# VectorE's order in the last two steps: the maximum of tile 31 behind the low parts of tile 29, the multiply of tile 31 behind the low parts of tile 30

## The chip, the cores and the metric

The kernel runs on one core of one Trainium2 chip. The metric is the device time in microseconds of one execution; before the change its median is 170.57 over three runs (170.32 to 170.78).

## The reference

The input x is 4 images of 128 channels by 1024 pixels, float32. Two blocks follow each other, both with a residual:

```
L0 (no softmax):  g, theta = W x + b  (64 channels)     phi = W x + b  (64 channels)
                  y = (theta^T phi / 1024) g            x1 = x + out_w y + out_b
L1 (attention):   theta, phi = W x1 + b  (128 channels)
                  attn = softmax(theta^T phi / sqrt(128))   over the 1024 pixels
                  out = x1 + conv1_w (attn x1) + conv1_b
```

## The kernel before, in words

L0 has no softmax, so the kernel folds it into one affine map per image (jobs pg, MT, R, A), and Z = x1 comes from one product (job Z). In L1 the weights of theta and phi are joined (job t makes the queries), and conv1 is multiplied into the values (job V), so that the attention yields the result but for bias and residual.

Every product that needs float32 accuracy is done in parts: a tensor is split into a high part (rounded to fp32r) and a low part (the rest), and three products high x high, high x low, low x high are added up (`three`, L220). ScalarE or GpSimd make the high parts, VectorE most of the low ones.

The attention runs in ALL = 32 tiles of 128 rows, 8 for each image, numbered 0 to 31 through the four images. For tile n these steps follow, each on its engine:

1. TensorE: scores (L223 to L225) into `ring[:, n % 2]`, two banks for each of two tiles.
2. VectorE: `row_max` (L680), the negated maximum of each row of `ring`.
3. GpSimd: `row_shift` (L821), adds a row term: the shift of the exponentials. 128x1 elements.
4. ScalarE: `exps` (L523), exponentials with their row sums, into one of 4 buffers P.
5. VectorE: `norm` (L686 and L688), reciprocal of the sums and the multiply of P, 128x1024 in place.
6. TensorE: `turn` (L318), eight transposes of 128x128 into `turned`, in two halves. It waits for `norm` of its tile and, for each half, for the low parts of the tile before (`turned` is a single buffer).
7. ScalarE: `high_turned` (L531), the high part of each half.
8. VectorE: `low_turned` (L695), the low part of each half: `turned` less the high part.
9. TensorE: `attend` (L338), for each group of four tiles, 24 products of 512 columns in four pieces, spread over the steps behind.

There is no scheduler: the order on each engine is the order in which its function issues instructions, and semaphores with constant counts join the engines. Each engine has a loop over n = 0 to 30, called steps here. A step n holds scores of tile n + 2 and transposes of tile n on TensorE; maximum of n + 2, norm of n + 1 and low parts of n on VectorE; high copies of n and then exponentials of n + 2 on ScalarE; shift of n + 2 on GpSimd. In the last image no work for a next image is left between them.

The end differs from the rest. Behind the last pieces of group 6, TensorE waits for both low parts of tile 30 and does `attend_last` for the 384 columns of tiles 28 to 30 (L345, three products for each of 8 chunks): the first two chunks, then the transposes of tile 31, then the other six. Tile 31 itself is not split into parts; it is copied once (L627 by ScalarE, L775 by VectorE) and multiplied in plain float32 (L467). `finish_last` (L703) adds bias and Z, and two DMAs store the last results. ScalarE copies the sums of group 6 (`copy_numer`, L541) behind the high copies of tile 30, and GpSimd's `finish` (L837) adds Z to that copy, 128x512, and a DMA stores it.

Of the kernel before, what the change touches and what calls it, by code (L numbers as in the profile page):

```python
# [18 lines left out]
ALL = IMAGES * TILES  # L19
# [55 lines left out]
def build(nc, x, pg_weights, pg_bias, inner, weights, out):  # L75
    with ExitStack() as ctx:
# [85 lines left out]
        def columns(half):  # L162
            return slice(half * BANK, (half + 1) * BANK)

        def half_chunks(half):
            return slice(half * CHUNKS_PER_HALF, (half + 1) * CHUNKS_PER_HALF)
# [465 lines left out]
        def _(dve):  # L632
# [21 lines left out]
            def low_t(b, half):  # L654
                dve.wait_ge(aux_high, high_after(b, f"t{half}"))
                nc.vector.scalar_tensor_tensor(out=t_lo[:, b % 2, columns(half)], in0=aux[:, :], scalar=u,
                                               in1=t_hi[:, b % 2, columns(half)].bitcast(F32), op0=ALU.add,
                                               op1=ALU.subtract).then_inc(aux_free, 1)
# [18 lines left out]
            def row_max(n):  # L677
                b, t = divmod(n, TILES)
                dve.wait_ge(scores_ready, n + 1)
                nc.vector.tensor_reduce(negmax[:, t:t + 1], ring[:, n % 2, :], AX.X, ALU.max,  # L680
                                        negate=True).then_inc(max_ready, 1)

            def norm(n):
                t = n % TILES
                dve.wait_ge(probs_ready, n + 1)
                nc.vector.reciprocal(rden[:, t:t + 1], den[:, t:t + 1]).then_inc(rden_ready, 1)  # L686
                dve.wait_ge(rden_ready, n + 1)
                nc.vector.tensor_scalar(P[:, n % P_BUFFERS, :], P[:, n % P_BUFFERS, :],  # L688
                                        rden[:, t:t + 1], None, ALU.mult).then_inc(probs_normed, 1)

            def low_turned(n, half):
                group, k = divmod(n, GT)
                rows = slice(k * TILE, (k + 1) * TILE)
                dve.wait_ge(turned_hi, n * HALVES + half + 1)
                nc.vector.tensor_tensor(PT_lo[:, group % GROUPS, half_chunks(half), rows],  # L695
                                        turned[:, columns(half)].rearrange("p (j r) -> p j r", j=CHUNKS_PER_HALF),
                                        PT_hi[:, group % GROUPS, half_chunks(half), rows].bitcast(F32),
                                        ALU.subtract).then_inc(turned_lo, 1)
# [42 lines left out]
            def early_job(b, t):  # L741
                if t == 0 and b > 1:
                    make_pg(b, 0)
                if t == 2:
                    low_A(b)
                if t == 4:
                    low_t(b, 0)
                if t == 5:
                    low_V(b, 1)
                if t == 6:  # L750
                    low_t(b, 1)

            def late_job(b, t):
                if t == 0 and b > 1:
                    make_pg(b, 1)
                if t == 4:
                    low_V(b, 0)
                if t == 5:
                    low_V(b, 2)

            for n in range(ALL - 1):
                b, t = divmod(n, TILES)
                if t and b + 1 < IMAGES:
                    late_job(b + 1, t - 1)
                if n + 2 < ALL:
                    row_max(n + 2)
                if n == 0:
                    low_t(0, 1)
                norm(n + 1)
                if n and b + 1 < IMAGES:  # L770
                    early_job(b + 1, t)
                low_turned(n, 0)
                low_turned(n, 1)
            dve.wait_ge(turned_ready, ALL * HALVES)
            nc.vector.tensor_copy(PT_last[:, half_chunks(1), :], turned[:, columns(1)].rearrange(  # L775
                "p (j r) -> p j r", j=CHUNKS_PER_HALF)).then_inc(last_turned[1], 1)
# [129 lines left out]
```

## Time and profile before

| | |
|---|---|
| median of three runs | 170.57 us |
| profiled execution, its own time | 170.84 us |
| its span | 169.0 us |
| TensorE busy (matmul) | 161.8 us, 96% |
| VectorE busy | 124.1 us, 73% |
| ScalarE busy | 95.8 us, 57% |
| GpSimd busy | 69.1 us, 41% |
| granted TensorE clock | full in all 40 slices |

The span runs from the first to the last instruction that the profiler records on the core; the execution's own time is 1.84 us longer. Busy shares are averages over the whole kernel. The ends of matmuls are modelled, so starts are the better measure on TensorE.

### The profile page before, as it was taken

What the parts mean: (1) busy time and instruction counts of PE and PEld (TensorE: products, weight loads), DVE (VectorE), ACT (ScalarE), POOL (GpSimd) and SP (SyncE); (2) the same over time, 40 slices, a digit from 0 to 9 for tenths busy, and PEclk for the clock granted to TensorE, in tenths of its full rate; (3) what the DMA queues carried; (4) which work ended last, traced back from release to release, by engine and by line L of the source; (5) the groups of instructions that cost most, each with busy time, mean ns of one, the idle gap of its engine ahead of it and who ended that gap; (6) DMA issues with size and microseconds to landing.
All of it is one profiled execution on the core that took longest, in us unless ns stands there. A gap on an engine that the chain in (4) does not pass through costs nothing.

```text
span 169.0 us, 2605 instructions
## 1 busy us (share of the span) xinstructions
PE 161.8 (96%) x967; PEld 135.2 (80%) x967; DVE 124.1 (73%) x211; ACT 95.8 (57%) x181; POOL 69.1 (41%) x79
## 2 busy tenths in 40 slices
PE   7889899799999999999999999999999999998994
PEld 7777778687888887887888888887888888886893
DVE  1316599869888876867888987667888898888412
ACT  3024558769557546567557656467566766576410
POOL 1009765277102295236415296216525253825030
PEclk9999999999999999999999999999999999999999
DMA  4603030000000010000001010000000110000111
GB/s 134 207 0 128 0 124 0 0 0 2 6 0 0 4 62 0 0 0 4 0 0 47 17 66 0 0 0 4 0 2 0 63 49 17 0 0 0 62 63 65
DMA packets 2829, 4.76 MB, mean 28 GB/s; under 512 B 448, under 2 KB 1280, under 8 KB 2816
## 3 DMA queue, kind: packets, MB, share of 16 engines
q1 hardware_dynamic: 2304, 4.39, 7.5%
q10 hardware_dynamic: 512, 0.20, 0.5%
q8 instruction: 8, 0.13, 0.3%
q14 instruction: 5, 0.04, 0.1%
HBM read 2.49 MB, written 2.10 MB: 27 GB/s over the span
## 4 chain that ended last, share of the span: by engine, by line
PE 84%; DVE 7%; DMA 3%; ACT 2%; POOL 2%; issue 1%; SPq 0%; ACTq 0%
PE numer L338 22%; PE turned L318 14%; PE ring L223 9%; PE ring L225 8%; PE ring L224 8%; PE aux L282 4%; DMA X<-x_dram 3%; DVE negmax L680 3%; PE aux L229 3%; PE aux L345 2%; PE aux L235 2%; PE aux L223 2%; DVE P L688 2%; ACT P L523 1%; PE aux L225 1%; PE aux L224 1%
## 5 line engine op out<-in xcount | busy, mean ns | idle before, releaser
L821 POOL TENSOR_SCALAR shift<-negmax,rho 128x1 f32<-128x1 f32 x32 | 27.6, 863 | 72.8 <-DVE negmax L680 69.8
L680 DVE TENSOR_REDUCE negmax<-ring 128x1 f32<-128x1024 f32 x32 | 39.1, 1223 | 19.0 <-PE ring L225 18.8
L523 ACT ACTIVATE P<-ring,shift 128x1024 f32<-128x1024 f32 x32 | 35.8, 1119 | 9.9 <-POOL shift L821 9.8
L695 DVE TENSOR_TENSOR PT_lo<-turned,PT_hi 128x512 fp32r<-128x512 f32 x62 | 39.7, 681 | 0.4 <-ACT PT_hi L531 0.4
L531 ACT ACTIVATE PT_hi<-turned 128x512 fp32r<-128x512 f32 x62 | 33.6, 595 | 9.4 <-PE turned L318 9.3
L318 PE MATMUL turned<-identity,P 128*128 128x128 f32 x256 | 33.6, 274 | 0.6 <-DVE PT_lo L695 0.6
L318 PEld LDWEIGHTS turned<-identity,P 128*128 128x128 f32 x256 | 29.5, 141 | 3.9 <-DVE P L688 1.0
L223 PE MATMUL ring<-Z_hi,t_hi 128*128 128x512 f32 x64 | 26.5, 414 | 0.9 <-DVE t_lo L725 0.7
L225 PE MATMUL ring<-Z_lo,t_hi 128*128 128x512 f32 x64 | 25.2, 394 | 0.0
L224 PE MATMUL ring<-Z_hi,t_lo 128*128 128x512 f32 x64 | 25.2, 393 | 0.0
L688 DVE TENSOR_SCALAR P<-P,rden 128x1024 f32<-128x1024 f32 x32 | 24.1, 754 | 1.1
L338 PE MATMUL numer<-PT_hi,V_hi 128*128 128x512 f32 x56 | 24.4, 436 | 0.0
L338 PE MATMUL numer<-PT_hi,V_lo 128*128 128x512 f32 x56 | 22.1, 394 | 0.0
L338 PE MATMUL numer<-PT_lo,V_hi 128*128 128x512 f32 x56 | 22.1, 394 | 0.0
L223 PEld LDWEIGHTS ring<-Z_hi,t_hi 128*128 128x128 f32 x64 | 12.0, 188 | 4.1 <-DVE t_lo L725 1.0
L225 PEld LDWEIGHTS ring<-Z_lo,t_hi 128*128 128x128 f32 x64 | 12.0, 188 | 2.7
L224 PEld LDWEIGHTS ring<-Z_hi,t_lo 128*128 128x128 f32 x64 | 12.1, 188 | 2.2
L338 PEld LDWEIGHTS numer<-PT_hi,V_lo 128*128 128x128 f32 x56 | 10.5, 188 | 2.6
L338 PEld LDWEIGHTS numer<-PT_lo,V_hi 128*128 128x128 f32 x56 | 10.6, 190 | 1.3
L338 PEld LDWEIGHTS numer<-PT_hi,V_hi 128*128 128x128 f32 x56 | 10.6, 189 | 1.3
L837 POOL TENSOR_TENSOR result<-attended,Z 128x512 f32<-128x512 f32 x7 | 9.0, 1292 | 4.2 <-ACT attended L541 4.2
L503 ACT ACTIVATE t_hi<-aux,U 128x512 fp32r<-128x512 f32 x7 | 4.8, 688 | 8.1 <-PE aux L225 8.0
(117 smaller groups left out, 202.1 us busy)
## 6 DMA issues: line engine op xcount, KB each, us to landing
out_dram<-result SPq DMA_DIRECT2D x7, 256.0 KB, 2.0
X<-x_dram SPq DMA_DIRECT2D x3, 512.0 KB, 3.3
X<-x_dram SPq DMA_DIRECT2D x2, 256.0 KB, 4.2
out_dram<-result SPq DMA_DIRECT2D x1, 192.0 KB, 1.9
w<-weights_dram SPq DMA_DIRECT2D x1, 128.0 KB, 5.5
wi<-inner_dram ACTq DMA_DIRECT2D x1, 64.2 KB, 5.7
pg_w<-pg_weights_dram ACTq DMA_DIRECT2D x1, 64.0 KB, 3.3
pg_b<-pg_bias_dram ACTq DMA_DIRECT2D x1, 64.0 KB, 5.5
```

Of the source, the lines that this page charges most:

```text
L223: nc.tensor.matmul(to, left_hi, right_hi[:, cols], start=first, stop=False)
L224: nc.tensor.matmul(to, left_lo, right_hi[:, cols], start=False, stop=False)
L225: return nc.tensor.matmul(to, left_hi, right_lo[:, cols], start=False, stop=last)
L318: mm = nc.tensor.transpose(turned[:, j * TILE:(j + 1) * TILE], P[:, n % P_BUFFERS, j * TILE:(j + 1) * TILE], identity[:, :])
L338: mm = nc.tensor.matmul(numer[:, :], left[:, b % 2, chunk], right[:, g, j, :], start=(j == 0 and n == 0), stop=(j == TILES - 1 and n == 2))
L523: nc.scalar.activation(P[:, n % P_BUFFERS, :], ring[:, n % 2, :], ACT.Exp, bias=shift[:, t:t + 1], accum_out=den[:, t:t + 1]).then_inc(pro ...
L531: nc.scalar.activation(PT_hi[:, group % GROUPS, half_chunks(half), k * TILE:(k + 1) * TILE], turned[:, columns(half)].rearrange("p (j r) - ...
L680: nc.vector.tensor_reduce(negmax[:, t:t + 1], ring[:, n % 2, :], AX.X, ALU.max, negate=True).then_inc(max_ready, 1)
L688: nc.vector.tensor_scalar(P[:, n % P_BUFFERS, :], P[:, n % P_BUFFERS, :], rden[:, t:t + 1], None, ALU.mult).then_inc(probs_normed, 1)
L695: nc.vector.tensor_tensor(PT_lo[:, group % GROUPS, half_chunks(half), rows], turned[:, columns(half)].rearrange("p (j r) -> p j r", j=CHUN ...
L821: nc.gpsimd.tensor_scalar(shift[:, t:t + 1], negmax[:, t:t + 1], rho[:, b % 2, t:t + 1], rho[:, b % 2, t:t + 1], ALU.subtract, ALU.add).th ...
L837: nc.gpsimd.tensor_tensor(result[:, g, :], attended[:, g, :], Z[:, b % Z_BUFFERS, columns(g)], ALU.add).then_inc(result_ready, 1)
```

## The change

In step 29 VectorE's maximum of tile 31 moves from the front to the end of the step, behind the low parts of tile 29. In step 30 the norm of tile 31 moves behind the low parts of tile 30. The other engines are not edited.

```diff
--- before.py
+++ after.py
@@ -762,15 +762,19 @@
                 b, t = divmod(n, TILES)
                 if t and b + 1 < IMAGES:
                     late_job(b + 1, t - 1)
-                if n + 2 < ALL:
+                if n + 2 < ALL - 1:
                     row_max(n + 2)
                 if n == 0:
                     low_t(0, 1)
-                norm(n + 1)
+                if n + 1 < ALL - 1:
+                    norm(n + 1)
                 if n and b + 1 < IMAGES:
                     early_job(b + 1, t)
                 low_turned(n, 0)
                 low_turned(n, 1)
+                if n + 2 == ALL - 1:
+                    row_max(n + 2)
+            norm(ALL - 1)
             dve.wait_ge(turned_ready, ALL * HALVES)
             nc.vector.tensor_copy(PT_last[:, half_chunks(1), :], turned[:, columns(1)].rearrange(
                 "p (j r) -> p j r", j=CHUNKS_PER_HALF)).then_inc(last_turned[1], 1)
```

VectorE, the end of its queue, the new order against the one before (L680 maximum, L686 and L688 norm, L695 the two low parts of one tile, L775 the copy of tile 31); the first L695 is that of tile 28:

```order
 L695 TENSOR_TENSOR PT_lo<-turned,PT_hi 128x4x128 x2
-L680 TENSOR_REDUCE negmax<-ring 128x1
 L686 RECIPROCAL rden<-den 128x1
 L688 TENSOR_SCALAR P<-P,rden 128x1024
 L695 TENSOR_TENSOR PT_lo<-turned,PT_hi 128x4x128 x2
+L680 TENSOR_REDUCE negmax<-ring 128x1
+L695 TENSOR_TENSOR PT_lo<-turned,PT_hi 128x4x128 x2
 L686 RECIPROCAL rden<-den 128x1
 L688 TENSOR_SCALAR P<-P,rden 128x1024
-L695 TENSOR_TENSOR PT_lo<-turned,PT_hi 128x4x128 x2
-L775 COPY PT_last<-turned 128x512
+L779 COPY PT_last<-turned 128x512
```

The first L680 (tile 31) has moved behind the norm of tile 30 and the low parts of tile 29; the low parts of tile 30 have moved ahead of the last L686 and L688 (tile 31).

ScalarE, the end of its queue in the new kernel, the same as before (L531 the two high copies of one tile, L523 exponentials, L541 the copy of group 6, L627 the copy of tile 31); the first row is that of tile 29:

```order
111 L531 ACTIVATE PT_hi<-turned 128x4x128 x2
112 L523 ACTIVATE P,den<-ring,shift 128x1024
113 L531 ACTIVATE PT_hi<-turned 128x4x128 x2
114 L541 ACTIVATE attended<-numer,bias 128x512
115 L627 ACTIVATE PT_last<-turned 128x512
```

Nothing moved here: exponentials of tile 31 stand between the high copies of tile 29 and those of tile 30.

## Rows read from the trace of the kernel before

**Rows 1.** The page, part 4: share of the ending chain by engine.

```profile
PE 84%; DVE 7%; DMA 3%; ACT 2%; POOL 2%; issue 1%; SPq 0%; ACTq 0%
```

**Rows 2.** Chain that ended last, 135 to 169 us: start us, us, what.

```profile
152.92 1.22 DVE negmax L680
...
154.25 0.75 DVE P L688
155.01 0.61 DVE PT_lo L695
...
156.92 2.81 PE numer L338 x12
...
166.58 0.35 DVE result L703
```

**Rows 3.** Timeline of PE, 145 to 169: start us, us, instruction [idle before].

```profile
154.77 0.40 PE L338 MATMUL numer<-PT_hi,V_lo 128*128 128x512 f32 x1
155.75 1.17 PE L318 MATMUL turned<-identity,P 128*128 128x128 f32 x8 [0.59 <-DVE PT_lo L695]
...
159.56 0.34 PE L345 MATMUL aux<-PT_hi,V_hi 128*128 128x384 f32 x1
...
160.60 1.04 PE L318 MATMUL turned<-identity,P 128*128 128x128 f32 x8
161.40 0.42 PE L345 MATMUL aux<-PT_hi,V_hi 128*128 128x384 f32 x1
161.65 0.33 PE L345 MATMUL aux<-PT_lo,V_hi 128*128 128x384 f32 x1
```

**Rows 4.** Timeline of DVE, 14 to 37 and 145 to 169.

```profile
25.46 0.75 DVE L688 TENSOR_SCALAR P<-P,rden 128x1024 f32<-128x1024 f32 x1
...
28.64 0.75 DVE L688 TENSOR_SCALAR P<-P,rden 128x1024 f32<-128x1024 f32 x1
...
156.69 0.75 DVE L688 TENSOR_SCALAR P<-P,rden 128x1024 f32<-128x1024 f32 x1
157.36 1.28 DVE L695 TENSOR_TENSOR PT_lo<-turned,PT_hi 128x512 fp32r<-128x512 f32 x2
```

**Rows 5.** Timeline of ACT, 140 to 169.

```profile
151.67 1.12 ACT L523 ACTIVATE P<-ring,shift 128x1024 f32<-128x1024 f32 x1 [0.83 <-POOL shift L821]
...
153.36 1.08 ACT L531 ACTIVATE PT_hi<-turned 128x512 fp32r<-128x512 f32 x2 [0.49 <-PE turned L318]
155.25 1.11 ACT L523 ACTIVATE P<-ring,shift 128x1024 f32<-128x1024 f32 x1 [0.81 <-POOL shift L821]
...
156.42 1.14 ACT L531 ACTIVATE PT_hi<-turned 128x512 fp32r<-128x512 f32 x2
159.82 0.69 ACT L541 ACTIVATE attended<-numer,bias 128x512 f32<-128x512 f32 x1 [2.27 <-PE numer L338]
```

**Rows 6.** Timeline of all engines, 64 to 66.

```profile
64.62 1.09 ACT L531 ACTIVATE PT_hi<-turned 128x512 fp32r<-128x512 f32 x2 [0.37 <-PE turned L318]
...
65.25 1.29 DVE L695 TENSOR_TENSOR PT_lo<-turned,PT_hi 128x512 fp32r<-128x512 f32 x2 [0.21 <-ACT PT_hi L531]
```

**Rows 7.** Timeline of POOL, 14 to 169.

```profile
24.80 0.37 POOL L821 TENSOR_SCALAR shift<-negmax,rho 128x1 f32<-128x1 f32 x1 [0.95 <-DVE negmax L680]
...
28.71 0.92 POOL L821 TENSOR_SCALAR shift<-negmax,rho 128x1 f32<-128x1 f32 x1 [0.47 <-DVE negmax L680]
...
154.25 0.91 POOL L821 TENSOR_SCALAR shift<-negmax,rho 128x1 f32<-128x1 f32 x1 [2.67 <-DVE negmax L680]
...
160.59 1.28 POOL L837 TENSOR_TENSOR result<-attended,Z 128x512 f32<-128x512 f32 x1 [4.19 <-ACT attended L541]
```

**Rows 8.** Line L821, all and from 18 to 28; line L688: ns min/median/max.

```profile
L821 POOL TENSOR_SCALAR shift<-negmax,rho x32: 359/914/925, 19.4 to 154.2; 128x1 f32<-128x1 f32 x32
...
L821 POOL TENSOR_SCALAR shift<-negmax,rho x3: 359/366/371, 19.4 to 24.8; 128x1 f32<-128x1 f32 x3
...
L688 DVE TENSOR_SCALAR P<-P,rden x32: 752/754/756, 21.3 to 156.7; 128x1024 f32<-128x1024 f32 x32
```

## The prediction

> **What bounds the kernel now.** I read the page's chain first: TensorE holds 84% of it and VectorE 7% [rows 1]. The chain in order of time then shows where TensorE is not the bound, since the change touches only the last two of 31 steps. Up to the maximum of tile 31 the last steps are all TensorE; there the chain leaves it for the first time: row maximum of tile 31, multiply of tile 30, first low part of tile 29, and only then the transposes of tile 30 [rows 2]. From there it is TensorE without a gap until the last result. So two numbers matter: the start of the transposes of tile 30 and, since nothing later has slack, the start of those of tile 31. The last product of step 29 starts at 154.77 and the transposes at 155.75; products of this size follow each other every 0.23 (twelve in 2.81), so TensorE stood from 155.00, for 0.75 us [rows 2, 3]. The transposes of tile 31 start at 160.60 [rows 3]. The timelines of the other engines give what stands in between.
>
> **The change, part by part.** No instruction is added or removed; only VectorE's queue changes, and ScalarE, TensorE and GpSimd keep theirs.
>
> Part one, the maximum of tile 31 behind the multiply of tile 30 and the low parts of tile 29. The multiply of tile 30 now waits only for the exponentials of tile 30, which start at 151.67. In the one late case where VectorE waits for exponentials the multiply starts 1.44 behind their start (155.25 to 156.69) [rows 4, 5]. So it runs 153.11 to 153.86 instead of 154.25 to 155.00. The low parts of tile 29 need the high copy that starts at 153.36; where VectorE waits for such a copy it starts 0.63 behind its start (64.62 to 65.25) [rows 5, 6]. So 153.99, and at 1.28 for the pair [rows 4] they end at 155.27. The transposes of tile 30 then start at 155.00: the 0.75 us stall goes, and 0.1 of waiting between their halves. TensorE is done with the twelve products behind them some 0.85 early, near 158.6 (the two early groups of the last rows started at 159.56 [rows 3]).
>
> But this early arrival finds the next thing late. The maximum of tile 31 starts at 155.27 less 0.08, the overlap of neighbours on VectorE (156.69 + 0.75 against 157.36 [rows 4]), 155.19, against 152.92: 2.27 us late. Its duration is 1.22, then 0.11 to GpSimd's shift (154.25 less 154.14) [rows 2, 7]. What the shift costs is the first unknown. All 32 are the same 128x1 instruction, and last 359 to 925 ns with the median at 914; the three of the first 28 us that are short last 359 to 371. The one at 24.80 (0.37) ends before the multiply at 25.46; that at 28.71 (0.92) lies beside the multiply of 28.64, as the one at 154.25 lies beside the multiply that starts with it [rows 4, 7, 8]. In the new order the shift of tile 31 has no multiply beside it, since the multiply of tile 30 is long done. I take 0.37, and 0.92 as the other end. The exponentials start 0.03 to 0.09 behind it (0.09 at 155.25, after a shift from 154.25 of 0.91 [rows 5, 7]; I take 0.03 for a short shift, an estimate), so at 155.19 + 1.22 + 0.11 + 0.37 + 0.03 = 156.92, against 155.25.
>
> On ScalarE the high copies of tile 30 stand behind the exponentials of tile 31, in both kernels. That is the point the whole matter turns on. From the start of exponentials to the start of the high copies behind it: 156.42 less 155.25, 1.17 [rows 5]. TensorE's transposes may have set part of this, and I take 1.14: 158.06. Then 0.63 to the low parts of tile 30: 158.69, and 1.28: 159.97. TensorE's last rows wait for both of these low parts, and start 0.13 behind (first low part of tile 29, 155.01 + 0.61, to 155.75 [rows 2, 3]): 160.10 against 159.56, which is **+0.54**. After a wait the first product of this size takes 0.25 to the next where the others take 0.17 (161.40 and 161.65) [rows 3]: **+0.08**. So the gain of 0.85 at TensorE's front is kept by nothing; it becomes a stall of about 1.5 us, from 158.6 to 160.1.
>
> Part two, the low parts of tile 30 ahead of the multiply of tile 31. Before, the multiply ran at 156.69, 3.9 us ahead of the transposes that need it. Now it can start 0.11 behind the low parts, as that at 154.25 started 0.11 behind the maximum (the reciprocal fits in between), at 160.08, and end at 160.83, with 0.13 at 160.96; the transposes of tile 31 are reached at 160.10 + 1.04 (159.56 to 160.60) + 0.08 = 161.22. Alone it would fit with 0.26 to spare. But it has new company. ScalarE copies the numerators behind the high copies: 158.06 + 1.08 less 0.1 of overlap = 159.04, for 0.69, and GpSimd's sum starts 0.08 behind (159.82 + 0.69 to 160.59) [rows 5, 7]: 159.81 to 161.09, across the start of the multiply. What the two do to each other is the second unknown. The rows show multiplies of 752 to 756 ns, all 32, while the shift beside them is lengthened by 0.55 [rows 8]. The lengthened one ends just behind the multiply: 155.16 against 155.00 and 29.63 against 29.39 [rows 2, 4, 7]. So it waits for the multiply's end and doesn't only run slower. In these overlaps the multiply starts first or together with the shift, so nothing shows who yields when GpSimd is well ahead. Bounds: no wait for the multiply, or the whole rest of the sum, 161.09 less 160.08, 1.01. I take that the second one waits, as it does in the rows. Then the multiply ends at 161.09 + 0.75 = 161.84 at most, and the transposes start at 161.97, against 160.60: +1.37. The shift of 154.25 ends 0.16 behind its multiply and takes 0.37 alone, so 0.21 of an instruction can lie beside the other; that gives +1.16. I take **+1.3**, of which 0.62 is part one.
>
> The rule of the Trainium skill that speaks against this change stands in "SBUF — State Buffer", section "Who interferes with whom": VectorE's two-port mode and GpSimd share one pair of ports as an exclusive lock, and whichever is first keeps it for its whole instruction. The trace agrees for VectorE first (0.92 against 0.37); no row shows GpSimd first. By the rule the sum is the +1.3 above; if VectorE always had precedence it would be +0.62.
>
> **The sum.** Nothing behind the transposes of tile 31 has slack to give back, as the chain is TensorE alone there [rows 2], and the output DMAs that the last steps wait for are earlier ones. Span 169.0 + 1.3 = 170.3; the profiled run took 170.84, 1.84 more than its span and 0.27 more than the median of 170.57. Against the run itself that is 172.1, against the median 171.9, which I forecast.
>
> **Rivals.**
> - The multiply doesn't wait for the sum on GpSimd: +0.62, so 171.2. For it: no multiply in 32 was ever lengthened. Against: none ever met GpSimd well under way.
> - The shift of tile 31 stays at 0.92 (its length has another cause): everything behind moves by 0.55, so +1.2 without and +1.9 with the wait for the sum: 171.8 to 172.5. Against it, the three short ones.
> - The other side, faster: the high copies of tile 30 start when their transposes are done (about 155.6) and not behind the exponentials. Then the low parts of tile 30 end at 155.6 + 0.63 + 1.28 = 157.5, the last multiply at 156.92 + 1.44 + 0.75 = 159.1, neither late for TensorE, whose groups run from 158.6 to 159.7: the transposes of tile 31 start 0.9 earlier than at 160.60, so 169.7. It decides from the point where ScalarE takes the copies first; its queue holds them second, and every row of ScalarE stands in the order of its queue.
> - TensorE's clock falls in the new stalls (1.5 and 0.7 us). It was granted in full in every slice, across the wait of 0.75 too. What remains of TensorE work from 159.56 on is 7.0 us (to the last result's 166.58 [rows 2, 3]); all of it at half the clock would add up to 7, a part of it some 1 to 3: 173 to 178.
> - The change does nothing, because the two edits cancel or the low parts of tile 30 are early enough: 170.6. They would have to end by 159.43, 0.54 earlier than worked out, and the multiply would have to be free too.
>
> **How the numbers follow.** Forecast with the wait on the ports 0.56, multiply free 0.24, long shift 0.07, clock 0.03, nothing 0.05, faster 0.05. What counts as a difference is 0.3%, 0.51 us. The forecast, the long shift and the clock are slower for certain (0.66); the free multiply lies at +0.62, close above the bound, and gives 0.16 to slower and 0.08 to the middle. So slower 0.82, same 0.13, faster 0.05. The range: the forecast's own is 171.5 to 172.3; it reaches down to the free multiply, less 0.2 for the spread of medians, 171.0, and up to the long shift with its wait, 172.5. I leave out the clock, the faster case and the middle.
>
> **What would show it.** In the changed profile: transposes of tile 30 at 155.0, no wait ahead of them; multiply of tile 30 at 153.1; shift of tile 31 at 0.37 from about 156.5; exponentials at 156.9; high copies of tile 30 at 158.1; a TensorE wait of 1.5 us for the low parts ahead of the first 384-column product, at 160.1; the last multiply beside GpSimd's sum, with a recorded time of well over 0.75 or a late start, and a second wait ahead of the transposes of tile 31, at about 161.9. Wrong it would be if the last multiply keeps 0.75 and its start (then the free case), if the shift takes 0.9, or if the high copies of tile 30 begin before the last exponentials.

## The result, and the profile after

The changed kernel takes 171.47 us (median of 6 runs, 171.22 to 171.85) where the kernel before takes 170.47 us (median of 6 on the same chip): a ratio of 1.0057, 95% interval 1.0032 to 1.0082. It is 1.0 us slower. The forecast was 171.9 in a range of 171.0 to 172.5, with a chance of 0.82 for slower.

The head of the page of the profiled run, which took 171.54 us:

```profile
span 169.7 us, 2605 instructions
```

This span is only 0.7 us over the 169.0 of before, for the most part because the run had a quicker start: the products that wait for the second half of the first image begin at 5.98, against 6.50, which is 0.52 us. The transposes of tile 29 start at 152.15 now; before they started at 152.72, as the one row of TensorE's timeline of before says that was not shown yet:

```profile
152.72 1.04 PE L318 MATMUL turned<-identity,P 128*128 128x128 f32 x8
```

So the two traces are compared from that start on, 0.57 us apart. From the transposes of tile 29 to those of tile 31 it was 152.72 to 160.60, 7.88 us, before [rows 3]; now it is 152.15 to 161.14, 8.99 us: +1.11. The rest, from there to the last result, is 6.04 us now (161.14 to 167.18) and was 5.98 (160.60 to 166.58) [rows 2, 3].

The chain that ended last, in order of time (start us, us, what):

```profile
155.94 0.38 POOL shift L825
...
156.41 1.21 ACT P L523 x2
...
158.13 1.29 DVE PT_lo L695 x2
...
159.53 1.57 DVE P L688
...
161.14 1.09 PE turned L318 x8
...
167.18 0.35 DVE result L703
```

Where the chain of before was TensorE alone from the transposes of tile 30 on [rows 2], it now leads through every engine: shift, exponentials and high copy of the last tiles, the two low parts of tile 30, the last multiply, and only then TensorE again. Its 1.57 us for the multiply are the line to stop at.

TensorE's timeline; the first two groups are the transposes of tiles 29 and 30:

```profile
152.15 1.04 PE L318 MATMUL turned<-identity,P 128*128 128x128 f32 x8
...
154.43 1.03 PE L318 MATMUL turned<-identity,P 128*128 128x128 f32 x8
...
159.48 0.44 PE L345 MATMUL aux<-PT_hi,V_hi 128*128 128x384 f32 x1 [1.22 <-DVE PT_lo L695]
159.76 0.34 PE L345 MATMUL aux<-PT_lo,V_hi 128*128 128x384 f32 x1
...
161.14 1.09 PE L318 MATMUL turned<-identity,P 128*128 128x128 f32 x8 [0.35 <-DVE P L688]
```

The stall ahead of the transposes of tile 30 is gone: they follow 2.28 us behind those of tile 29, against 3.03 before (152.72 to 155.75 [rows 3]). In its place stand two others: 1.22 us ahead of the first 384-column product, which waits for the low parts, and 0.35 us ahead of the transposes of tile 31, which wait for the multiply. Measured from start to start, and less the usual distance of two products, they are 1.39 us (157.86 to 159.48, less 0.23) and 0.52 us (160.45 to 161.14, less 0.17). The product behind the first stall comes 0.28 us later and not 0.17.

VectorE, in its new order (multiply and low parts, maximum; then low parts and multiply), answering to [rows 4]:

```profile
152.53 0.76 DVE L688 TENSOR_SCALAR P<-P,rden 128x1024 f32<-128x1024 f32 x1
153.42 1.29 DVE L695 TENSOR_TENSOR PT_lo<-turned,PT_hi 128x512 fp32r<-128x512 f32 x2
154.63 1.21 DVE L680 TENSOR_REDUCE negmax<-ring 128x1 f32<-128x1024 f32 x1
158.13 1.29 DVE L695 TENSOR_TENSOR PT_lo<-turned,PT_hi 128x512 fp32r<-128x512 f32 x2 [2.29 <-ACT PT_hi L531]
...
159.53 1.55 DVE L688 TENSOR_SCALAR P<-P,rden 128x1024 f32<-128x1024 f32 x1
```

ScalarE, answering to [rows 5]:

```profile
156.41 1.12 ACT L523 ACTIVATE P<-ring,shift 128x1024 f32<-128x1024 f32 x1 [2.53 <-POOL shift L825]
...
157.51 1.07 ACT L531 ACTIVATE PT_hi<-turned 128x512 fp32r<-128x512 f32 x2
158.47 0.70 ACT L541 ACTIVATE attended<-numer,bias 128x512 f32<-128x512 f32 x1
```

GpSimd, the shifts of tiles 30 and 31 and the sum of group 6, answering to [rows 7]:

```profile
150.09 0.92 POOL L825 TENSOR_SCALAR shift<-negmax,rho 128x1 f32<-128x1 f32 x1 [2.83 <-DVE negmax L680]
155.94 0.37 POOL L825 TENSOR_SCALAR shift<-negmax,rho 128x1 f32<-128x1 f32 x1 [4.94 <-DVE negmax L680]
...
159.24 1.29 POOL L841 TENSOR_TENSOR result<-attended,Z 128x512 f32<-128x512 f32 x1 [1.66 <-ACT attended L541]
```

The maximum ends near 155.84, the shift of tile 31 lasts 0.37 us with no multiply beside it (that of tile 30, 0.92), and the exponentials start at 156.41, with the high copies 1.10 us behind them. The sum runs from 159.24 to 160.53. The last multiply starts at 159.53, within it, and lasts 1.55 us, twice its usual 0.75.

### The profile page after: what moved, and what is told of

Its sections match the earlier page's. It is cut to its first block, busy times and chain, and to the rows that moved or that the text cites. A ratio compares the mean times of both kernels' runs of the same rounds, so it can differ in the third digit from the quotient of the medians.

```text
span 169.7 us, 2605 instructions
## 1 busy us (share of the span) xinstructions
PE 161.3 (95%) x967; PEld 134.5 (79%) x967; DVE 125.0 (74%) x211; ACT 95.7 (56%) x181; POOL 68.6 (40%) x79
## 4 chain that ended last, share of the span: by engine, by line
PE 78%; DVE 8%; issue 4%; ACT 3%; DMA 3%; POOL 2%; SPq 0%; ACTq 0%; POOLq 0%
PE numer L338 19%; PE turned L318 13%; PE ring L223 8%; PE ring L225 8%; PE ring L224 8%; PE aux L282 4%; DVE negmax L680 3%; DMA X<-x_dram 3%; PE aux L229 3%; PE aux L235 2%; DVE P L688 2%; ACT P L523 2%; PE aux L345 2%; PE aux L223 2%; DVE PT_lo L695 1%
## 5 line engine op out<-in xcount | busy, mean ns | idle before, releaser
L825 POOL TENSOR_SCALAR shift<-negmax,rho 128x1 f32<-128x1 f32 x32 | 27.0, 845 | 75.0 <-DVE negmax L680 72.1
L680 DVE TENSOR_REDUCE negmax<-ring 128x1 f32<-128x1024 f32 x32 | 39.1, 1223 | 18.5 <-PE ring L225 18.3
L523 ACT ACTIVATE P<-ring,shift 128x1024 f32<-128x1024 f32 x32 | 35.8, 1120 | 11.6 <-POOL shift L825 11.5
L695 DVE TENSOR_TENSOR PT_lo<-turned,PT_hi 128x512 fp32r<-128x512 f32 x62 | 39.7, 681 | 2.8 <-ACT PT_hi L531 2.7
L531 ACT ACTIVATE PT_hi<-turned 128x512 fp32r<-128x512 f32 x62 | 33.6, 595 | 9.4 <-PE turned L318 9.3
L688 DVE TENSOR_SCALAR P<-P,rden 128x1024 f32<-128x1024 f32 x32 | 24.9, 778 | 1.1
```

The costliest lines, as they stand in the source:

```text
L523: nc.scalar.activation(P[:, n % P_BUFFERS, :], ring[:, n % 2, :], ACT.Exp, bias=shift[:, t:t + 1], accum_out=den[:, t:t + 1]).then_inc(pro ...
L531: nc.scalar.activation(PT_hi[:, group % GROUPS, half_chunks(half), k * TILE:(k + 1) * TILE], turned[:, columns(half)].rearrange("p (j r) - ...
L825: nc.gpsimd.tensor_scalar(shift[:, t:t + 1], negmax[:, t:t + 1], rho[:, b % 2, t:t + 1], rho[:, b % 2, t:t + 1], ALU.subtract, ALU.add).th ...
```

## The experiments

All are timed against the kernel before on the same chip, the nine experiments in five rounds with 4 to 12 executions of each kernel. The middle column is taken from each profile: the time from the start of the transposes of tile 29 to that of tile 31 on TensorE, less the 7.88 us of before. It leaves out the start, in which the first loads differ from run to run.

| kernel | in the trace, us | median, us | before, us | ratio (95% interval) |
|---|---|---|---|---|
| the change | +1.11 | 171.47 | 170.47 | 1.0057 (1.0032 to 1.0082) |
| 1, maximum late only | +0.97 | 171.51 | 170.54 | 1.0058 (1.0044 to 1.0073) |
| 2, low parts first only | +0.02 | 170.47 | 170.54 | 0.9997 (0.9987 to 1.0007) |
| 3, sum behind the multiply | +0.59 | 171.28 | 170.54 | 1.0039 (1.0026 to 1.0053) |
| 4, high copies first | -0.87 | 169.59 | 170.54 | 0.9944 (0.9930 to 0.9957) |
| 5, high copies first, VectorE as before | +1.43 | 172.14 | 170.49 | 1.0093 (1.0080 to 1.0106) |
| 6, sum in four pieces | +0.60 | 171.04 | 170.49 | 1.0041 (1.0023 to 1.0059) |
| 7, as 4, norm first | +0.96 | 171.48 | 170.49 | 1.0053 (1.0040 to 1.0066) |
| 8, a multiply beside the shift | +1.53 | 172.38 | 170.49 | 1.0126 (1.0093 to 1.0158) |
| 9, high copies and low parts first, maximum early | +0.02 | 170.49 | 170.44 | 0.9999 (0.9987 to 1.0012) |

**1. Part one alone.** Against the changed kernel:

```diff
-                if n + 1 < ALL - 1:
-                    norm(n + 1)
+                norm(n + 1)
...
-            norm(ALL - 1)
```

> Part one alone: the maximum of tile 31 stands behind the low parts of tile 29, the multiply of tile 31 stays ahead of the low parts of tile 30. Theory (the late maximum holds up ScalarE, whose high copies of tile 30 stand behind the exponentials of tile 31): the low parts of tile 30 now wait for the multiply of tile 31 as well, 1.44 behind the start of the exponentials, and end some 0.4 us later than in the changed kernel, so the first 384-column product waits some 0.4 us longer; but the multiply runs before GpSimd's sum starts and keeps 0.75 us, so there is no second wait. Together +1.0 us against the kernel before, as much as the whole change. Rival (part two is what costs, by its wait for GpSimd's sum): at most half of the loss, +0.2 to +0.5 us.

Measured: +0.97 in the trace, +0.97 by the medians. The end of VectorE's queue, multiply of tile 31 and low parts of tile 30:

```profile
158.39 0.75 DVE L688 TENSOR_SCALAR P<-P,rden 128x1024 f32<-128x1024 f32 x1
159.06 1.28 DVE L695 TENSOR_TENSOR PT_lo<-turned,PT_hi 128x512 fp32r<-128x512 f32 x2
```

and TensorE behind it, the first 384-column product and the transposes of tile 31:

```profile
160.40 0.44 PE L345 MATMUL aux<-PT_hi,V_hi 128*128 128x384 f32 x1 [1.57 <-DVE PT_lo L695]
...
161.55 1.03 PE L318 MATMUL turned<-identity,P 128*128 128x128 f32 x8
```

The multiply keeps 0.75 us, since it comes ahead of the sum; the low parts stand behind it, and the one wait is 1.57 us instead of 1.22 and 0.35. So part one alone costs what the whole change costs. The rival, that part two is to blame, falls.

**2. Part two alone.** Against the changed kernel:

```diff
-                if n + 2 < ALL - 1:
+                if n + 2 < ALL:
                     row_max(n + 2)
...
-                if n + 2 == ALL - 1:
-                    row_max(n + 2)
```

> Part two alone: the maximum of tile 31 at the front of its step as before, the low parts of tile 30 ahead of the multiply of tile 31. Theory: the stall ahead of the transposes of tile 30 stays (0.75 us), the low parts of tile 30 start at most 0.3 us earlier, where they have slack of 0.8 us, and the multiply ends 2 us or more ahead of its transposes and of GpSimd's sum at 0.75 us: 0.0 us against the kernel before, within 0.2. Rival (part two costs by itself): +0.3 us or more.

Measured: +0.02 in the trace, and no difference by the runs. TensorE, transposes of tiles 29, 30 and 31:

```profile
152.23 1.04 PE L318 MATMUL turned<-identity,P 128*128 128x128 f32 x8
...
155.26 1.16 PE L318 MATMUL turned<-identity,P 128*128 128x128 f32 x8 [0.59 <-DVE PT_lo L695]
...
160.13 1.04 PE L318 MATMUL turned<-identity,P 128*128 128x128 f32 x8
```

The stall of 0.59 us by the record (0.75 from start to start) is as before [rows 3], and nothing behind it waits. Part two is free as long as the maximum is early.

**3. The sum and the multiply apart.** Against the changed kernel:

```diff
+            pool.wait_ge(probs_normed, ALL)
             finish((IMAGES - 1) * GROUPS)
```

> The changed kernel, with GpSimd's sum of group 6 waiting for the last multiply, so that the two don't meet. Theory (the multiply lasts 1.55 us because GpSimd's sum was first at their common port): the multiply lasts 0.75 us, the wait ahead of the transposes of tile 31 goes, and the kernel is 0.4 to 0.5 us faster than the changed one, +0.5 to +0.65 us against the kernel before. Rival (the multiply is long for another reason, such as the copy or the transposes beside it): 1.55 us stays, +1.0 us.

Measured: +0.59 in the trace and +0.74 by the medians (0.0039, with 0.0026 to 0.0053, is 0.66 us). VectorE's last multiply, GpSimd's sum, and TensorE:

```profile
159.68 0.75 DVE L688 TENSOR_SCALAR P<-P,rden 128x1024 f32<-128x1024 f32 x1
```

```profile
160.52 1.28 POOL L841 TENSOR_TENSOR result<-attended,Z 128x512 f32<-128x512 f32 x1 [2.79 <-DVE P L688]
```

```profile
159.63 0.44 PE L345 MATMUL aux<-PT_hi,V_hi 128*128 128x384 f32 x1 [1.21 <-DVE PT_lo L695]
...
160.78 1.03 PE L318 MATMUL turned<-identity,P 128*128 128x128 f32 x8
```

The multiply lasts 0.75 us once the sum is moved away, and the transposes of tile 31 follow the two product groups without a wait. In the trace that is 0.52 us less than in the changed kernel. So the second of the two stalls comes from the sum, and the first, 1.21 us, is left as it was. Between the two kernels' own runs the gain is 0.2 us with intervals that overlap; the trace shows it, the times alone would not.

**4. ScalarE's order.** Against the changed kernel:

```diff
                 high_turned(n, 0)
                 high_turned(n, 1)
...
-                if n + 2 < ALL:
+                if n + 2 < ALL - 1:
                     exps(n + 2)
+            exps(ALL - 1)
```

> The changed kernel, with ScalarE's exponentials of tile 31 behind its high copies of tile 30. Theory (ScalarE's queue is what turned the early transposes into a loss): high copies of tile 30 right behind their transposes, low parts of tile 30 done 2 us earlier than in the changed kernel, last multiply at 0.75 us before GpSimd's sum, no wait of TensorE from the maximum of tile 31 to the end: 0.75 to 0.95 us faster than the kernel before, some 1.9 us faster than the changed one. Rival (the late maximum itself is too late, by the chain shift, exponentials, multiply to the transposes of tile 31): a wait of 0.5 us or more ahead of the transposes of tile 31, and 0.0 to -0.4 us against the kernel before.

Measured: -0.87 in the trace, -0.95 by the medians, ratio 0.9944 (0.9930 to 0.9957). This kernel, at 169.59 us, is faster than both. ScalarE, high copies of tile 30 and exponentials of tile 31; VectorE, low parts of tile 30 and multiply of tile 31; TensorE, transposes of tiles 29, 30 and 31:

```profile
155.38 1.09 ACT L531 ACTIVATE PT_hi<-turned 128x512 fp32r<-128x512 f32 x2 [1.19 <-PE turned L318]
156.72 1.12 ACT L523 ACTIVATE P<-ring,shift 128x1024 f32<-128x1024 f32 x1 [0.26 <-POOL shift L826]
```

```profile
156.08 1.28 DVE L696 TENSOR_TENSOR PT_lo<-turned,PT_hi 128x512 fp32r<-128x512 f32 x2
...
158.16 0.75 DVE L689 TENSOR_SCALAR P<-P,rden 128x1024 f32<-128x1024 f32 x1
```

```profile
152.47 1.04 PE L318 MATMUL turned<-identity,P 128*128 128x128 f32 x8
...
154.75 1.04 PE L318 MATMUL turned<-identity,P 128*128 128x128 f32 x8
...
159.48 1.03 PE L318 MATMUL turned<-identity,P 128*128 128x128 f32 x8
```

The copies now start at 155.38 behind their transposes, the low parts at 156.08, and TensorE waits for nothing from the maximum of tile 31 on. The gain that the change was missing is here in full: it had been made at the transposes of tile 30 and lost behind ScalarE's queue.

**5. ScalarE's order without VectorE's.** The kernel before with the edit of experiment 4.

> The kernel before with ScalarE's edit alone: exponentials of tile 31 behind the high copies of tile 30, VectorE's order as before. Theory (the two engines' orders only pay together): the stall of 0.75 us ahead of the transposes of tile 30 stays, since the maximum of tile 31 still stands ahead of their multiply; the exponentials now wait for the high copies, to 157.3, the multiply of tile 31 to 158.7, and the low parts of tile 30 stand behind it and end near 160.8, so the first 384-column product waits over 1 us: +1.3 us against the kernel before, at least +1.0. Rival (ScalarE's order is the gain of the fourth kernel, whatever VectorE does): -0.5 us or better.

Measured: +1.43 in the trace, +1.65 by the medians: slower than the change itself. ScalarE's copies and exponentials, and VectorE's multiply and low parts behind them:

```profile
156.36 1.13 ACT L531 ACTIVATE PT_hi<-turned 128x512 fp32r<-128x512 f32 x2 [1.97 <-PE turned L318]
157.39 1.11 ACT L523 ACTIVATE P<-ring,shift 128x1024 f32<-128x1024 f32 x1
```

```profile
158.82 0.75 DVE L689 TENSOR_SCALAR P<-P,rden 128x1024 f32<-128x1024 f32 x1
159.49 1.28 DVE L696 TENSOR_TENSOR PT_lo<-turned,PT_hi 128x512 fp32r<-128x512 f32 x2
```

The copies wait for the late transposes and push the exponentials from 155.25 to 157.39; the multiply waits for these, and the low parts for the multiply. Each order is a loss without the other.

**6. The sum in pieces.** Against the changed kernel, in `finish`, for group 6:

```diff
+                parts = 4 if group == ALL_GROUPS - 2 else 1
+                size = BANK // parts
+                for part in range(parts):
+                    cols = slice(part * size, (part + 1) * size)
...
+                op.then_inc(result_ready, 1)
```

> The changed kernel with GpSimd's sum of group 6 cut into four instructions of 128 columns. Theory (the port is held for one instruction at a time, first come first served): the last multiply waits for one piece only, at most 0.45 us, and lasts 0.8 to 1.2 us; the wait ahead of the transposes of tile 31 shrinks to 0.15 us or nothing, +0.55 to +0.8 us against the kernel before, 0.2 to 0.4 us faster than the changed kernel. Rival (GpSimd keeps the port as long as its next instruction is queued): the multiply lasts 1.8 us or more, +1.3 us or more.

Measured: +0.60 in the trace, +0.55 by the medians. VectorE's multiply, and the first three pieces on GpSimd:

```profile
161.32 0.76 DVE L688 TENSOR_SCALAR P<-P,rden 128x1024 f32<-128x1024 f32 x1
```

```profile
161.03 0.45 POOL L845 TENSOR_TENSOR result<-attended,Z 128x128 f32<-128x128 f32 x1 [1.67 <-ACT attended L541]
...
161.44 0.95 POOL L845 TENSOR_TENSOR result<-attended,Z 128x128 f32<-128x128 f32 x1
...
```

The multiply starts at 161.32, in the last 0.16 us of the first piece, and is not lengthened at all, where 0.8 to 1.2 us was expected. The second piece, queued directly behind the first, lasts 0.95 us where the others last 0.45: it is the one that waited, for the multiply's end at 162.08. So GpSimd doesn't keep VectorE out because its next instruction is queued. How long a multiply would wait that starts in the middle of a piece, no run shows. One place in the trace of before has the same picture, a multiply that starts in the last 0.03 us of a GpSimd sum, with a shift behind that sum:

```profile
37.51 0.75 DVE L688 TENSOR_SCALAR P<-P,rden 128x1024 f32<-128x1024 f32 x1
```

```profile
36.26 1.28 POOL L829 TENSOR_TENSOR Z_lo<-Z,Z_hi 128x512 fp32r<-128x512 f32 x1
37.52 0.89 POOL L821 TENSOR_SCALAR shift<-negmax,rho 128x1 f32<-128x1 f32 x1
```

There too the multiply keeps 0.75 us, and the shift pays. That the tail of an instruction doesn't hold the other up is seen in the changed kernel too: the multiply ends 0.55 us behind the sum, not 0.75. By the runs' own times the interval overlaps that of the changed kernel, so the gain over it is read from the trace.

The profiled run of this kernel took 172.78 us, 1.7 more than its median, and that has nothing to do with the sum. Its products for the second half of the first image waited 1.54 us and began at 6.78, only 0.28 us later than in the trace of before (6.50, after 0.62 us). But the granted clock, 1.0 up to there, was 0.67 of full from 6.78 to 8.30, 0.50 (the lower level, 1.2 GHz) from 8.30 to 10.00, and 1.0 again from 11.00. By the products of L251 the run was 1.19 us late (10.77 against 9.58). The trace column leaves this out, and from 150 us on the clock is 1.0.

**7. Part two on top of experiment 4 taken back.** Experiment 4 with the edit of experiment 1.

> The fourth kernel (exponentials of tile 31 behind the high copies of tile 30, maximum late) without part two: the multiply of tile 31 ahead of the low parts of tile 30. Theory (with early copies the low parts must not stand behind a multiply that waits for the exponentials): low parts end near 160.3, the first 384-column product waits 1.7 us, +0.8 to +1.0 us against the kernel before, 1.8 us slower than the fourth kernel. Rival (part two is worth nothing, as in the second kernel): -0.95 us as the fourth.

Measured: +0.96 in the trace, +0.99 by the medians. VectorE's multiply of tile 31 and low parts of tile 30:

```profile
158.15 0.75 DVE L689 TENSOR_SCALAR P<-P,rden 128x1024 f32<-128x1024 f32 x1
158.82 1.28 DVE L696 TENSOR_TENSOR PT_lo<-turned,PT_hi 128x512 fp32r<-128x512 f32 x2
```

The high copies start at 155.37 here as well, but the low parts stand behind the multiply to 158.82, 2.7 us later than in experiment 4. Part two, which is worth nothing alone, is worth 1.8 us once the rest is in place.

**8. A multiply beside the shift.** Against the changed kernel:

```diff
                     row_max(n + 2)
+                    nc.vector.tensor_scalar(X[:, 0, :], X[:, 0, :], bias[:, B_C:B_C + 1], None, ALU.mult)
```

> The changed kernel with one more VectorE multiply of 128x1024 float32 (on an image buffer that nobody reads any more, by a per-row factor as the real one) right behind the maximum of tile 31, so that it runs beside the shift of tile 31, with VectorE idle there otherwise. Theory (the shift lasts 0.9 and not 0.37 us only where a multiply has the common port): the shift of tile 31 is 0.9 us again, and everything behind moves by 0.55 us: +1.5 to +1.6 us against the kernel before. Rival (the short shift has another cause): 0.37 us and +1.0 us as the changed kernel.

Measured: +1.53 in the trace; by the medians +1.89, with the two longest of six runs at 173.6 and 173.8. VectorE's added multiply and the last one, and GpSimd's shift of tile 31:

```profile
155.74 0.75 DVE L777 TENSOR_SCALAR X<-X,bias 128x1024 f32<-128x1024 f32 x1
...
159.93 1.55 DVE L688 TENSOR_SCALAR P<-P,rden 128x1024 f32<-128x1024 f32 x1
```

```profile
155.92 0.80 POOL L826 TENSOR_SCALAR shift<-negmax,rho 128x1 f32<-128x1 f32 x1 [4.93 <-DVE negmax L680]
```

The shift lasts 0.80 and not 0.37 us; it ends 0.23 us behind the added multiply, as it ended 0.16 and 0.24 us behind the real ones [rows 4, 7]. Everything behind it is 0.42 us later than in the changed kernel. The long shift is the multiply's doing. The last multiply, which meets the sum 0.28 us after the sum's start (159.65), lasts 1.55 us again. The rest of the time by the medians is scatter that I can't assign: the trace is that of the shortest run, 171.86 us.

**9. The two orders without the late maximum.** Experiment 2 with ScalarE's edit of experiment 4.

> The last of the subsets of the three edits: low parts of tile 30 ahead of the multiply of tile 31 on VectorE, high copies of tile 30 ahead of the exponentials of tile 31 on ScalarE, the maximum of tile 31 at the front of its step as before. Theory (the maximum's place alone decides on the stall ahead of the transposes of tile 30, the two others only on what comes behind): the stall of 0.75 us stays; high copies at 156.4, low parts of tile 30 from 157.0 to 158.3, exponentials at 157.4, multiply of tile 31 from 158.8 to 159.6 at 0.75 us, all ahead of TensorE's first 384-column product at 159.6 and of the transposes at 160.6: 0.0 us against the kernel before, within 0.2. Rival (part of the fourth kernel's gain comes from the early copies by themselves): -0.3 us or better.

Measured: +0.02 in the trace, and no difference by the runs. TensorE, transposes of tiles 29, 30 and 31:

```profile
152.58 1.04 PE L318 MATMUL turned<-identity,P 128*128 128x128 f32 x8
...
155.61 1.16 PE L318 MATMUL turned<-identity,P 128*128 128x128 f32 x8 [0.59 <-DVE PT_lo L696]
...
160.48 1.03 PE L318 MATMUL turned<-identity,P 128*128 128x128 f32 x8
```

The stall ahead of the transposes of tile 30 is back and nothing else waits. With the low parts first, the early copies cost nothing, and gain nothing either: it is the late maximum that takes the stall away, and the other two edits that keep what it gives.

## Why the prediction was right

The times below are given in the clock of before, so 0.57 us are added to those of the changed kernel.

- The transposes of tile 30 at 155.00: measured 154.43 + 0.57 = 155.00. TensorE's last product before the first stall is 0.89 us early (159.32 before, 158.43 now), where I had 0.85.
- The shift of tile 31 alone, 0.37 us: measured 0.37, and experiment 8 shows the cause.
- Exponentials at 156.92 and high copies at 158.06: 156.98 and 158.08. Here small errors cancel, which is luck: the exponentials start 0.10 us behind the end of the shift and not 0.03, the high copies 1.10 behind the exponentials and not 1.14, and TensorE starts 0.06 behind the low parts and not 0.13.
- ScalarE's queue as the point on which it turns: experiment 4 changes only that, and turns +1.11 into -0.87. The rival with the other sign named exactly this condition, and its -0.9 was what it gives; what was wrong with it as a forecast is that the changed kernel doesn't contain it.
- The first term, +0.54 and +0.08: the first 384-column product is at 160.05 against 159.56, +0.49; the restart is 0.28 less 0.17, +0.11. The 0.08 that I had for it came from a row that I misread: the product at 161.40 stands behind transposes, without a wait, and is followed after 0.25 us. That a stall costs nearly the same is luck. Together +0.60 for +0.62, and experiment 3, where only these are left, has +0.59.
- The second term, the wait of the last multiply for the sum: the sum at 159.81 (measured 159.81), the multiply at 160.08 (160.10) to 161.84 at most (161.65). The mechanism was right, the size was 0.2 us too large: I took +1.3 between +1.16 and +1.37, and it is +1.11, 0.05 under the lower of the two. Two things make it smaller. The multiply needed to wait only until 0.2 us before the recorded end of the sum, which the +1.16 had in it; and TensorE started 0.06 us behind the multiply (159.53 + 1.55 to 161.14), where I had 0.13.
- The rule of "SBUF — State Buffer" in the Trainium skill, section "Who interferes with whom", that whichever is first keeps the shared ports for its whole instruction, had no row in the trace of before with GpSimd well ahead; the nearest is the multiply at 37.51, in the last 0.03 us of a sum (shown at experiment 6), which the prediction passed over. The last multiply (1.55 us) is such a row, and experiments 3 and 8 agree with the rule but for the end: by the record the second is held up to a point some 0.2 us before the end of the instruction in front, and in experiment 6 a multiply that starts 0.16 us before that end is not held. There the measurement decides.
- The rival of a free multiply (+0.62) is what experiments 3 and 6 show, when the sum is moved or cut. The rival of a falling clock didn't come: the granted clock stayed at the upper level (1.0) across both stalls, and across the 1.57 and 1.64 us of experiments 1 and 8. It isn't an empty rival, though: in the profiled run of experiment 6 the clock fell behind a wait of 1.54 us near the start.

The medians give +1.0 and the trace +1.11; the interval of the ratio, 0.5 to 1.4 us, holds both.

## What to carry to other kernels

Earlier work on the bounding engine is worth nothing before the queue of each engine behind it has been followed to the place where its result is taken up: here 0.9 us gained on TensorE turned into a loss of 1.1 us because the instruction that was moved late stood, through two more engines, ahead of the next copy in ScalarE's queue. A reordering is one edit over all queues: the three edits of the fastest kernel are worth -0.87 us together, while each of the six smaller subsets of them changes nothing or costs 1.0 to 1.4 us. And an instruction that is moved gets new neighbours in time; where VectorE's SBUF-to-SBUF multiply and a GpSimd instruction met in these runs, the later one paid unless the first was in its last 0.16 us, so the longer one should be kept off the path or cut.

## What the runs showed of the hardware that I had not expected

- A multiply that starts 0.29 us into a GpSimd sum of 128x512 lasts 1.55 us instead of 0.75 (0.28 us into it, in experiment 8, 1.55 too), but one that starts in the last 0.16 us of a GpSimd instruction is not lengthened at all (0.76).
- With GpSimd's sum in four pieces the multiply started at the end of the first piece, and the second, queued behind it, lasted 0.95 us instead of 0.45: a queue of GpSimd instructions doesn't keep VectorE out.
- The first product behind a stall is followed by the next in 0.28 or 0.29 us where the others take 0.17, after stalls of 1.2 to 1.6 us, at an unchanged clock. Behind transposes, without a stall, it is 0.25 or 0.26.
- A wait of 1.54 us ahead of 6.78 was followed by a granted clock of 0.67 and then 0.50 up to 10.00 (experiment 6), while waits of 1.57 and 1.64 us near the end left it at 1.0. What makes the difference, these runs don't show.
